# A recommendation tower on one core: four more fields selected by one-hot products, gathers spaced out, and the layers around the last grams in another order

## What is computed

```python
e = jnp.stack([tbl_0[ids[:, 0]], ..., tbl_31[ids[:, 31]]], axis=1)      # 2048 x 32 x 64
gram = jnp.einsum('bnd,bmd->bnm', e, e)
z = gram[:, rows, cols]                                                 # rows < cols: 496
h = jnp.concatenate([z, dense_ctx], axis=1)                             # 2048 x 512
h = jnp.maximum(h @ W_top1 + b_top1, 0.0)                               # 512
h = jnp.maximum(h @ W_top2 + b_top2, 0.0)                               # 256
y = h @ W_top3                                                          # 1
```

## Time and profile before

| | |
|---|---|
| median of 3 runs | 456.71 us (453.65 to 462.18) |
| the profiled execution | 457.0 us, of which 455.2 us are the span of the profile |
| TensorE, products | 362.1 us busy, 80% of the span |
| TensorE, loading weights | 286.6 us, 63% |
| GpSimd | 245.3 us, 54% |
| VectorE | 181.7 us, 40% |
| ScalarE | 116.6 us, 26% |
| mean granted clock of TensorE | 0.914 of 2.4 GHz |

### The profile page before, as it was taken

The page is one execution under the profiler, slowest core; times in us unless marked ns, Lnnn a source line. Parts: engine busy times, 40 slices in busy tenths (PEclk is TensorE's granted clock), DMA queues, the critical chain, the costliest instruction groups (busy, mean ns, idle before and its releaser), DMA issues.

```text
span 455.2 us, 16612 instructions
## 1 busy us (share of the span) xinstructions
PE 362.1 (80%) x7652; PEld 286.6 (63%) x7652; DVE 181.7 (40%) x545; ACT 116.6 (26%) x148; POOL 245.3 (54%) x264
## 2 busy tenths in 40 slices
PE   0787878596699989988899899897999898674057
PEld 0676767585488955864888757745889543554045
DVE  3899996052078720430578502601774000000000
ACT  4224252221222222303232123113222221230002
POOL 3777777777777777777777777777700000000000
PEclk9999989587599999999899999987999999897559
DMA  7848222111388511111778211114850015100610
GB/s 233 285 113 279 53 71 53 32 29 29 57 154 182 174 29 30 27 30 31 133 151 232 52 29 29 27 29 70 152 109 1 4 23 68 46 1 4 88 48 0
DMA packets 38847, 36.29 MB, mean 80 GB/s; under 512 B 14645, under 2 KB 27767, under 8 KB 38650
## 3 DMA queue, kind: packets, MB, share of 16 engines
q1 hardware_dynamic: 30298, 25.78, 24.9%
q0 software_dynamic: 8192, 8.40, 8.9%
q10 hardware_dynamic: 288, 1.05, 0.7%
HBM read 27.14 MB, written 8.07 MB: 77 GB/s over the span
## 4 chain that ended last, share of the span: by engine, by line
PE 71%; DVE 11%; issue 7%; ACT 5%; DMA 4%; SPq 3%; PEldq 0%; DVEq 0%
PE sel_ps L439 33%; PE tower_ps L485 14%; PE gram_ps L471 12%; DVE onehot L405 7%; PE tower_ps L494 7%; PE gat_ps L456 4%; PE tower_ps L503 2%; ACT work L296 2%; DVE work L389 2%; ACT vecs L282 2%; DVE tabs L394 1%; DMA work<-products 1%; DMA ids_wide<-ids_scratch 1%; DMA sel_ids<-in_ids_sel_dram 1%; SPq L167 1%
## 5 line engine op out<-in xcount | busy, mean ns | idle before, releaser
L255 POOL DMA_INDIRECT rows<-in_tbl_dram,gat_ids x256 | 244.4, 955 | 83.3 <-issue 77.4
L405 DVE TENSOR_SCALAR onehot<-ids_wide,row_ids 128x512 bf16<-128x512 f16 x528 | 162.9, 375 | 159.2 <-PE sel_ps L439 155.2
L439 PE MATMUL sel_ps<-onehot,tabs 128*64 128x256 bf16 x3168 | 191.2, 283 | 28.6 <-DVE onehot L405 15.7
L439 PEld LDWEIGHTS sel_ps<-onehot,tabs 128*64 128x64 bf16 x3168 | 178.4, 114 | 38.9 <-issue 21.7
L485 PE MATMUL tower_ps<-work,w_sb 128*128 128x512 f32 (+1 forms) x160 | 62.7, 546 | 21.0 <-DMA work<-products 20.9
L471 PE MATMUL gram_ps<-vecs 64*32 64x32 f32 x4096 | 53.1, 211 | 28.1 <-issue 17.9
L471 PEld LDWEIGHTS gram_ps<-vecs 64*32 64x32 f32 x4096 | 44.9, 113 | 47.0 <-issue 36.5
L282 ACT COPY vecs<-sel_ps 128x512 f32<-128x512 f32 x32 | 33.5, 1066 | 100.1 <-PEq L448 92.5
L485 PEld LDWEIGHTS tower_ps<-work,w_sb 128*128 128x128 f32 x160 | 32.2, 208 | 41.8 <-DMA work<-products 21.2
L287 ACT COPY vecs<-gat_ps 128x512 f32<-128x512 f32 x32 | 33.3, 1074 | 31.8 <-PE gat_ps L456 31.8
L296 ACT COPY work<-gram_ps 128x512 f32<-128x512 f32 x32 | 17.2, 589 | 60.8 <-PE gram_ps L471 60.8
(11 more groups left out here) (11 smaller groups left out, 6.4 us busy)
## 6 DMA issues: line engine op xcount, KB each, us to landing
ids_wide<-ids_scratch SPq DMA_DIRECT2D x32, 256.0 KB, 5.6
rows<-in_tbl_dram,gat_ids POOLq DMA_INDIRECT x256
products<-work SPq DMA_DIRECT2D x12, 248.0 KB
products<-work SPq DMA_DIRECT2D x24, 120.0 KB
work<-in_packed_dram SPq DMA_DIRECT2D x5, 512.0 KB, 6.2
work<-products SPq DMA_DIRECT2D x9, 256.0 KB
work<-in_packed_dram ACTq DMA_DIRECT2D x2, 512.0 KB, 4.4
w_sb<-in_w_dram SPq DMA_DIRECT2D x1, 1024.0 KB
```

The source lines that it names most:

```text
L255: nc.gpsimd.indirect_dma_start(out=rows[:, r, k, h, :], out_offset=None, in_=tables[GATHERED[k]], in_offset=bass.IndirectOffsetOnAxis(ap=g ...
L405: last = nc.vector.tensor_scalar(onehot[:, n % RING, c - c0, :], ids_wide[:, k, :], row_ids[chunks[k]][:, c:c + 1], None, ALU.is_equal)
L439: last = nc.tensor.matmul(sel_ps[DIM * h:DIM * h + DIM, g % 2, HALF * at:HALF * at + HALF], tabs[:, first_chunk[k] + c, part, :], onehot[: ...
```

## The change

- Four more fields (16, 21, 23, 29, of 1250 rows) are selected: 20 selected in 10 pairs, 12 gathered in 3 turns a round.
- A selection puts the two fields of a pair on the two column tiles, each for all 512 samples, in place of two halves of the samples. The one-hot pieces come in the order half 0 of both fields, half 1 of both. TensorE no longer waits for its own product; ScalarE waits for the last piece instead. ScalarE copies each pair in four copies of 64 x 256.
- The turns of round 0 follow the last three selections; before, they stood ahead of the last four.
- GpSimd: after most gathers three memsets of a spare column, each waiting for the one before (spacers); for the gathers in ALONE it waits instead until the gather has landed; gathers in GATES wait until a selection of the unit has used its first half: in units 2 and 3 the first waits for the first selection, the twelfth for the third.
- In units 1 and 2 layer 1 stands ahead of each gram chunk of round 0 instead of behind it; layer 2 is worked by output block, one block ahead of each of the first two chunks of round 1.
- In the last unit, layer 1 of unit 2 is cut in eight halves, one ahead of each gram chunk of both rounds. Layers 2 and 3 of unit 2 and all of pass 3 come behind the last gram.
- VectorE copies the last gram block of each unit (after the one-hots of the next unit's third pair) and half of two blocks of the last.
- SyncE stores unit 2's result behind both passes' reads; the ids of the selected fields are loaded by ScalarE's queue; z has a semaphore for even and one for odd passes.

The diff, cut to its core (`TURNS` was N_GAT // 4, `PAIRS` N_SEL // 2):

```diff
 N_SEL, N_GAT = len(SELECTED), len(GATHERED)
-PAIRS = N_SEL // 2
-TURNS = N_GAT // 4
...
@@ -39,17 +40,29 @@
 PASSES = [(u, 0, UNIT) for u in range(LAST)] + [(LAST, HALF * r, HALF) for r in range(ROUNDS)]
 MOVES = 3 * Q

+SPACERS = 3
...
+

 def gat_no(u, r, x):
-    return TURNS * (ROUNDS * u + r) + x
+    return N_TURNS * (ROUNDS * u + r) + x


 def emptied_no(u, r, b):
...
-                sp.dma_start(z[P - CTX:P, Q - 1, at], ctx_t[:, UNIT * u + x0:UNIT * u + x0 + width]).then_inc(z_in, 16)
+                    sp.wait_ge(h1_full, J1 * min(v, LAST))
...
-                if r == 0:
-                    store(LAST - 1)
                 rows_back(LAST + r)
+            store(LAST - 1)
...
+            def spacer():
+                n = next(count)
+                if n > 0:
+                    pool.wait_ge(spaced, n)
+                nc.gpsimd.memset(spare[:], 0.0).then_inc(spaced, 1)
+
...
+            def landed(u, r, x, k, h):
+                so_far = 2 * len(GROUPS[x]) * u + 2 * (k - GROUPS[x].start) + h + 1
+                pool.wait_ge(rows_in[r][x], 16 * so_far)

...
+                of_unit = [(r, x, k, h) for r in range(ROUNDS) for x in range(N_TURNS) for k in GROUPS[x] for h in range(2)]
+                for n, (r, x, k, h) in enumerate(of_unit):
+                    if u > 0 and k == GROUPS[x].start and h == 0:
+                        pool.wait_ge(gat_full, gat_no(u - 1, r, x) + 1)
+                    if n in GATES[u]:
+                        pool.wait_ge(onehot_used, piece_no(u, GATES[u][n], 0, 1) + 1)
+                    gather(u, r, x, k, h)
+                    if n in ALONE[u]:
+                        landed(u, r, x, k, h)
+                    else:
+                        for _ in range(SPACERS):
+                            spacer()
...
             def selected(u, g):
-                act.wait_ge(sel_full, PAIRS * u + g + 1)
-                at = N_GAT + 2 * g
-                nc.scalar.copy(vecs[:, :, at:at + 2].rearrange("p j f -> p f j"),
-                               sel_ps[:, g % 2, :].rearrange("p (f j) -> p f j", f=2)).then_inc(sel_emptied, 1)
+
+                act.wait_ge(onehot_used, piece_no(u, g, 1, 1) + 1)
+                for at in range(2):
+                    for h in range(2):
+                        last = nc.scalar.copy(vecs[DIM * h:DIM * h + DIM, :, N_GAT + 2 * g + at],
+                                              sel_ps[DIM * at:DIM * at + DIM, sel_no(u, g) % 2, HALF * h:HALF * h + HALF])
+                last.then_inc(sel_emptied, 1)

...
+                at, fields = GROUPS[x].start, len(GROUPS[x])
+                nc.scalar.copy(vecs[:, P * r:P * r + P, at:at + fields],
+                               gat_ps[:, n % 2, 0:P * fields].rearrange("p (f j) -> p j f", f=fields))\
+                  .then_inc(gat_emptied, 1)
...
+            def gram(u, r, b, halves):
...
+                for h in halves:
+                    nc.scalar.copy(gram_rows[:, r, h, :, 16 * b:16 * b + 16],
+                                   gram_ps[:, h, :, :].rearrange("p i m -> p m i")).then_inc(gram_emptied, 1)
...
+            act.dma_start(sel_ids[:], ids_sel).then_inc(sel_ids_in, 16)
...
+                if u == 0:
+                    act.wait_ge(w_in, 16 * 5)
+                else:
+                    layer1(u - 1, 0)
+                    if u < LAST:
+                        layer1(u - 1, 1)
+                gram(u, 0, 0, (0, 1))
...
+                for x in range(N_TURNS):
                     gathered(u, 1, x)
...
                 if u < LAST:
+
+                    act.wait_ge(gram_full, emptied_no(u, 1, 1) + 1)
                     selected(u + 1, 0)
                     selected(u + 1, 1)
-            for j in range(J1):
-                layer1(LAST + 1, j)
-            layer2(LAST + 1)
-            layer3(LAST + 1)
+                else:
+                    gram(u, 1, 1, (0,))
+            layer2(LAST - 1)
+            layer3(LAST - 1)
+            for v in (LAST, LAST + 1):
+                for j in range(J1):
+                    layer1(v, j)
+                layer2(v)
+                layer3(v)

...
+            def one_hots(u, g, half):
+                if half == 0:
+                    dve.wait_ge(wide_in[g], 16 * (u + 1))
+                for at in range(2):
+                    k, n = 2 * g + at, piece_no(u, g, half, at)
...
-                for k in range(N_SEL):
-                    one_hot(u, k)
+                for g in range(N_PAIRS):
+                    one_hots(u, g, 0)
+                    one_hots(u, g, 1)
+                    if g == 2:
+                        gram(u - 1, 1, 1, (0, 1))
+            for b in range(2):
+                gram(LAST, 1, b, (1,))
...
-                if PAIRS * u + g >= 2:
-                    pe.wait_ge(sel_emptied, PAIRS * u + g - 1)
+                n = sel_no(u, g)
+                if n >= 2:
+                    pe.wait_ge(sel_emptied, n - 1)
                 if u == 0:
...
+                last = [None, None]
+                for half in range(2):
+                    pe.wait_ge(onehot_ready, piece_no(u, g, half, 1) + 1)
+                    c0, c1 = halves[2 * g][half]
+                    for c in range(c0, c1):
+                        for part in range(PARTS):
+                            for at in range(2):
+                                k = 2 * g + at
+                                last[at] = nc.tensor.matmul(
+                                    sel_ps[DIM * at:DIM * at + DIM, n % 2, :], tabs[:, first_chunk[k] + c, part, :],
+                                    onehot[:, piece_no(u, g, half, at) % RING, c - c0, :],
+                                    start=(c == 0 and part == 0), stop=(c == chunks[k] - 1 and part == PARTS - 1),
+                                    skip_group_check=True)
+                    for at in range(2):
+                        last[at].then_inc(onehot_used, 1)
...
-                if j >= 2:
-                    pe.wait_ge(h1_ready, J1 * v + j - 1)
-                for c in range(Q):
-                    last = nc.tensor.matmul(tower_ps[:, j % 2, 0:width], w1_sb[:, c, P * j:P * j + P],
-                                            z[:, c, x0:x0 + width], start=(c == 0), stop=(c == Q - 1))
-                last.then_inc(h1_full, 1)
-
-            def layer2(v, part):
+                    if j >= 2:
+                        pe.wait_ge(h1_ready, J1 * v + j - 1)
...
+                if parts[-1] == 1:
+                    last.then_inc(h1_full, 1)
...
+                for j in range(J1):
+                    if o == 0:
+                        pe.wait_ge(h1_ready, J1 * v + max(j, 2) + 1)
+                    last = nc.tensor.matmul(tower_ps[:, (v + o) % 2, 0:width], w2_sb[:, j, P * o:P * o + P],
+                                            h1[:, j, 0:width], start=(j == 0), stop=(j == J1 - 1), skip_group_check=True)
+                last.then_inc(h2_full, 1)
...
-                    last = nc.tensor.matmul(tower_ps[0:1, 0, 0:width], w3_sb[:, o:o + 1], h2[:, o, 0:width],
+                    pe.wait_ge(h2_ready, J2 * v + o + 1)
...
             for u in range(UNITS):
-                select(u, 2)
-                select(u, 3)
-                for g in range(4, PAIRS):
-                    turn(u, 0, g - 4)
+                for g in range(2, N_PAIRS):
                     select(u, g)
+                    if g >= N_PAIRS - N_TURNS:
+                        turn(u, 0, g - N_PAIRS + N_TURNS)
                 if u == 1:
                     pe.wait_ge(w_in, 16 * 5)
                 for c in range(CHUNKS):
+                    if 0 < u < LAST:
+                        layer1(u - 1, c)
+                    if u == LAST:
+                        layer1(u - 1, c // 2, (c % 2,))
                     gram(u, 0, c)
-                    if u > 0:
-                        layer1(u - 1, c)
-                if u == LAST:
-                    layer2(u - 1, 0)
-                    layer2(u - 1, 1)
-                    layer3(u - 1)
                 turn(u, 1, 0)
                 turn(u, 1, 1)
                 if u < LAST:
                     select(u + 1, 0)
-                else:
-                    for j in range(J1):
-                        layer1(LAST, j)
-                    layer2(LAST, 0)
-                    layer2(LAST, 1)
-                    layer3(LAST)
                 turn(u, 1, 2)
                 if u < LAST:
                     select(u + 1, 1)
-                turn(u, 1, 3)
-                gram(u, 1, 0)
-                if 0 < u < LAST:
-                    layer2(u - 1, 0)
-                gram(u, 1, 1)
-                if 0 < u < LAST:
-                    layer2(u - 1, 1)
-                gram(u, 1, 2)
-                if 0 < u < LAST:
-                    layer3(u - 1)
-                gram(u, 1, 3)
-            for j in range(J1):
-                layer1(LAST + 1, j)
-            layer2(LAST + 1, 0)
-            layer2(LAST + 1, 1)
-            layer3(LAST + 1)
```

(23 more changed lines are left out.)

203 lines of the change are left out of this document (85 added, 118 removed).

## The result

| | before | changed kernel |
|---|---|---|
| median | 457.92 us (453.65 to 462.18, 4 runs) | 472.48 us (471.74 to 473.5, 4 runs) |
| ratio | | 1.0352 [1.0271, 1.0433] |
| profiled execution, its span | 457.0, 455.2 us | 471.7, 470.0 us |
| mean granted clock | 0.914 | 0.949 |

A forecast was written before the change was run, and what follows sets the result against it. TensorE's columns bound the middle, VectorE unit 0, and waits the end. +16 (unit 0) +16.8 (units 1, 2) +11.2 (unit 3) -32.8 (end) +6 (gathers) = +17.2: 474.2, said as 473 us, range 452 to 486.

The forecast's parts named there:

- signs of being right: Expected in the trace, among others: unit 0's last selection ends near 91 us; last selection to end 68 to 75 us.
- More selection: Selections on TensorE, third to last of a unit: 50.6 us instead of 39.4, +11.2 in each of units 1, 2, 3.
- Unit 0: VectorE's longer chain of one-hots and table parts in the first unit: +16 us, bounds +10 and +20.
- a quarter of it, 2 us, comes back: Unit 0's one-hots: of 8 us lost to gathers, rarer gathers (1.67 instead of 1.25 us apart) return 2 us.
- Copies: ScalarE's four copies per selection: 0.65 us each, some 2.3 in a row, hidden between selections; bounds 1.1 and 2.8.
- Layers ahead of the grams, units 1 and 2: Reordered layers and turns on TensorE: -2.8 us a unit; with the selections +8.4 a unit, 16.8 for two.
- The last unit: New order after the last selection: 68.2 us to the end against 101.0, so -32.8; bounds -38 and -24.
- Gathers in the last unit: Last gather lands at S+21.3, its turn wants it at S+15: +6 us, bounds 0 and +20.
- rival C: Gathers bind in the last unit through slower spacers (0.28 us) and landings (3.5 us): 490 us; chance 0.11.
- A: Rival: not slower, pacing frees more in one-hots, selections and grams: about 446 us, half of it 460; chance 0.25.
- B: Rival: spacer memsets on GpSimd hold up VectorE, +16 us, 489; decides from 0.06 us a memset on; chance 0.09.
- D: Rival: two fields' matmuls do not run side by side, a selection takes 10.2 us, total 670; chance 0.02.

The follow-up runs named there:

- a20_unpaced_b: Changed kernel without spacers, gates and waits for gathers' landings, on a third chip: 459.41 us, ratio 1.002 to the kernel before.
- a20_no_alone_b: Changed kernel in which no gather waits for its landing, spacers and gates kept, on a third chip: 456.85 us, ratio 0.996 to the kernel before.

## Why the prediction was right

The mechanism was right: more columns cost time, the new order at the end pays part of it back, and a wait for rows takes some of that away again. That the forecast came within 0.5 us is luck. In spans the parts are +9.4 to the third selection of unit 1, +19.0, +9.4, -23.0: +14.8, where the prediction had +16, +16.8, +11.2 and -26.8: +17.2. So two terms were 6.6 and 1.8 too high and two were 2.2 and 3.8 too low. The first lies outside its own bounds (+10 to +20), and two of the signs of being right failed: unit 0's selections ended at 87.0 and not near 91, and from S to the end it was 78.0 and not 68 to 75.

- *More selection.* Right. 48 matmuls took 5.37 us, 60 took 6.67 (5.55 and 6.7 taken), five selections in a row 28.3; from the third to the last 50.0, with 50.6 said: +9.4 for +11.2, near the lower bound of +9. Of the 1.8 us, 1.1 come from the kernel before, in which this stretch is 40.5 us long in unit 3 and not the 39.4 of unit 1.
- *Unit 0.* The step "a quarter of it, 2 us, comes back" was mis-sized. 91.4 was forecast for the last selection's end, and it was 87.0. Without pacing (a20_unpaced_b) it was 85.55 + 6.67 = 92.2, so the spacing gave back 5.2 us (4.1 by a20_no_alone_b, whose unit 0 is paced alike and ends its selections at 88.1). The rate of gathers alone, by which I had divided the 8 us, does not account for it: with three spacers behind each, a one-hot takes 0.29 us (8 in 2.32), with bare gathers 0.33 (8 in 2.63), so more than half of the excess over 0.264 goes, with gathers a quarter rarer. The rest up to the third selection was not a wash but 2.2 us shorter (43.9 against 46.1).
- *Copies.* Right: 605 ns each, 2.4 to 2.5 us for four, 2.67 ahead of unit 0's gram and 2.45 ahead of a third selection.
- *Layers ahead of the grams, units 1 and 2.* Units 1 and 2 took 19.0 more for 16.8 said. In it are 2.60 and 1.85 us of waiting for rows at each unit's last turn (210.14 and 315.12), where I had written "nobody waits". It is the mis-sized landing of the next point but one: in unit 2 the rows came at S+28.7 by that unit's own S (286.4, the end of its last selection) and were wanted at S+26.8; 21.3 and 28 had been the forecast's numbers. Without the two waits the term is 14.6, 2.2 below what was said.
- *The last unit.* -32.8 was right to 2 us. Without a wait for rows, S to the end took 66.4 and 66.2 us (a20_unpaced_b, a20_no_alone_b) against the 68.2 forecast. Inside it errors cancel in part: S to the last gram's end was 43.7 less 11.3, so 32.4, and not 28.3; from there to the end 34.3 and not 39.9, since a pass takes 11.7 us and not 14.3. Pass 4 did not wait for its products, as said, and the gaps of 2 us in the last gram, now with half layers between its chunks, shrank to 0.2 to 0.4 us.
- *Gathers in the last unit.* +6 was mis-sized: the wait was 11.33 us, over the 8 us that I had named as a sign of rival C. Of its terms, 29 x 1.67 = 48.4 held (48.2, from 347.26 to 395.42), but the gate opened at S-44.8 and not at S-47.1: the first gather behind it came 5.2 us after the third selection's start and not 3.5, since the first half took 4.5 us (granted clock 0.76 from 340 to 347 us) and 0.7 us passed before GpSimd went on. "2.5 us from one such gather to the next" was 3.0: eight from 395.42 to 419.32, of which the landings are 2.74 on the mean, and some 0.25 us lies between a landing and the next issue. The last lands at S+27.3, not S+21.3, and its turn was wanted at S+15.9. GpSimd in order of time, two of the lone gathers:

```profile
409.26 0.94 POOL L273 DMA_INDIRECT rows<-in_tbl_dram,gat_ids  x1 [1.77 <-DMA rows<-in_tbl_dram,gat_ids]
412.61 0.94 POOL L273 DMA_INDIRECT rows<-in_tbl_dram,gat_ids  x1 [2.41 <-DMA rows<-in_tbl_dram,gat_ids]
```

The rivals. A wanted third selections under 99 us apart, and they were 105.8 and 105.4. B falls by its own sign, one-hots above 0.35 us apart: in unit 0 they came nearer, to 0.29. The spacers themselves are slower beside one-hots. GpSimd of a20_no_alone_b in order of time, first beside one-hots, then with VectorE idle:

```profile
380.53 1.01 POOL L272 DMA_INDIRECT rows<-in_tbl_dram,gat_ids  x1
381.53 0.68 POOL L268 MEMSET spare<- 128x1 f32 x3
...
392.75 0.43 POOL L268 MEMSET spare<- 128x1 f32 x3
393.32 0.94 POOL L272 DMA_INDIRECT rows<-in_tbl_dram,gat_ids  x1
```

A gather with its spacers takes 1.72 us beside one-hots and 1.52 with VectorE idle, the three memsets 0.68 and 0.43 of it. Of the lock in the Trainium skill (SBUF — State Buffer, section "SBUF: two separate sides") these rows fit the half in which GpSimd waits; that the memsets hold up VectorE no row here shows, and whether the 0.03 us by which a one-hot still exceeds 0.264 are the gathers' or the memsets' was not taken apart. C was half true, in its landings and not in its spacers. Its sum was off besides: half of 27 us in the last unit and of 14 us in each of units 1 and 2, less the 6 counted already, come to some 495, not 490. D falls by 5.37 us a selection.

## What to carry to other kernels

Price a change in parts that each have a stage of their own, and look for the part that pays. Here the new order of layers in the last unit gave 19 to 32 us. Four more selected fields took 43, over 26 of them where TensorE was the bound and the rest mostly in unit 0, where VectorE was. Waits that pace a queue belong where nobody needs the last transfer: eight lone gathers ahead of the last turn cost 11 us, the same spacing without them nothing. Such a means against a disturbance wants a run where the disturbance is there: on one chip it cost 13 us, on another the kernel with spacers and gates took 498 us and the one without 617.
